# A GNN attention kernel on one core: a third of the probabilities is turned through DRAM and VectorE instead of TensorE

## The chip, the cores and the metric

One core of a Trainium2 chip. The metric is the device time of one launch in microseconds (us). PE is TensorE, DVE is VectorE, ACT is ScalarE, POOL is GpSimd, SP is SyncE, whose queue issues every DMA of this kernel.

## The reference, cut to what matters

`x` is (64, 128, 384) and `adj` (64, 128, 128), all float32; 12 heads of 32 columns.

```python
h = jnp.maximum(_layernorm(x, axis=-1), 0.0)
q, k, v = split_heads(h @ Wq + bq), split_heads(h @ Wk + bk), split_heads(h @ Wv + bv)
scores = jnp.einsum('bhqd,bhkd->bhqk', q, k) / jnp.sqrt(HD)
adj_e = adj[:, None, :, :]
scores = jnp.where(adj_e > 0, scores + beta * adj_e, -9e15)
probs = jax.nn.softmax(scores, axis=-1)
out = jnp.einsum('bhqk,bhkd->bhqd', probs, v)
x = x + out.transpose(0, 2, 1, 3).reshape(B, N, D)
```

## The kernel before, in words

The 64 graphs form 16 groups of four. The program of each engine is written out by hand as a chain of slots, one graph each, `s` = 0 to 3 inside a group; `Slot` says which works a slot does, and `slots` puts groups 2 to 11 in a hardware loop for PE, ACT, SP and POOL. Four graphs are in work in each slot: one is normalised (`z.t`), one gets scores and mask (`z.a`), the one before it is exponentiated and turned (`z.e = z.a - 1`), and the one before that is multiplied by v (`z.o = z.a - 2`). Besides, a share of the q and k projections of the whole group runs in every slot.

- **PE.** A matrix product for q and k is split into high and low parts: `h_hi*w_hi`, `h_hi*w_lo`, `h_lo*w_hi` for three pieces of the depth, nine matmuls of 512 columns for each of six units (`project`; `STRETCH_1` and `STRETCH_2` say which of them stand in which slot: 13, 14, 14 and 13). `values` is the same for v (nine of 384 columns). `scores` has 12 matmuls of depth 32 into the tile S_ps, `probs_times_v` has 12 into PT_ps, and `transpose_probs(z, m)`, m = 0, 1, 2, turns four heads each by four transposes into PT_ps. A slot runs `probs_times_v`, `scores`, `transpose_probs` 0, the first stretch, `values`, `transpose_probs` 1 and 2, the second stretch.
- **DVE.** `mask` adds the bias to the scores and takes the row maximum, 12 instructions with 12 reads of the accumulator. `store_outT` transposes the result in blocks of 32 and puts it in out_blocks, `transpose_blocks` does the same for the normalised graph, and `normalise`, `reciprocals`, `quotient` (y), `add_bv` (v), `moments`, `statistics`, `mask_terms`, `mask_bias`, `low_part` (h_lo) follow. `store_qk` moves two of six projection units from PSUM (`STORE_V`).
- **ACT.** `exponentials(z, m)`, four each for m = 0, 1, 2, with the row sum; `store_probsT(z, m)` copies the turned probabilities from PSUM to probsT; `high_part` (h_hi); `store_qk` for the other four units.
- **SP.** The tiles out_blocks and xhat_blocks go to DRAM in rows and come back in four reads each, which put the blocks of 32 where a 128 by 128 transpose has them. The queue works in order: a DMA whose semaphore is late keeps all behind it waiting. x is loaded a group at a time, in slot `s` = 1, and adj in slot `s` = 0.

Only for the first two groups (`z.X`) PE turns the normalised graph itself, and only in the last slots (`z.F`) it turns the output itself. The matmuls of `warm` keep PE busy while the first inputs arrive.

## Time and profile before

| what | value |
|---|---|
| median of 3 runs | 534.79 us (534.7 to 534.97) |
| the profiled execution's own time | 535.0 us |
| its span in the trace | 533.1 us |
| busy in the span: PE, ACT, DVE, POOL | 520.9, 462.3, 451.9, 127.3 us |
| granted TensorE clock | 1.0 of full speed |
| DMA: packets, bytes | 89671 packets, 75.25 MB |

The span is the time between the first and the last record. A busy time is the union of the instructions of an engine. Where instructions are pipelined, the mean duration of one is longer than the distance between two starts, and it is this distance that adds up.

### The profile page before, as it was taken

Reading aid. Unit: us, or ns where it says so; the run is one execution under the profiler, and the core shown is the slowest. Engines: PE = TensorE matmul, PEld = TensorE weight load, DVE = VectorE, ACT = ScalarE, POOL = GpSimd, SP = SyncE. Lnnn points to the kernel's source line nnn. Section 1 sums busy time; section 2 is a strip of 40 time slices with the busy share of each in tenths; the row PEclk is TensorE's granted clock in tenths of the full one; section 3 lists DMA queues with packets and bytes.
Section 4 is the critical chain, followed back from the end, with each engine's and each line's share of the span. In section 5 each row is a group of like instructions: output and inputs, shape, how many; then the busy total and the mean of one; then the engine's idle time right before and its main releaser. Section 6 shows DMA issues by size and latency. Waiting matters only on the chain.

```text
span 533.1 us, 17434 instructions
## 1 busy us (share of the span) xinstructions
PE 520.9 (98%) x5394; PEld 438.7 (82%) x5394; DVE 451.9 (85%) x2285; ACT 462.3 (87%) x1856; POOL 127.3 (24%) x204
## 2 busy tenths in 40 slices
PE   8989999999999999999999999999999999999995
PEld 8768888888888888888888888888888888888774
DVE  6788998888898898898888889888889987765896
ACT  3558899999999999999999999998998999888984
POOL 4522222212212222221221222222122111101211
PEclk9999999999999999999999999999999999999999
DMA  7523374654646465464645556364565434222111
GB/s 238 186 81 91 115 215 123 201 154 133 192 137 188 123 170 176 123 192 140 189 134 149 177 143 192 128 188 133 138 189 161 128 116 123 71 80 75 51 56 46
DMA packets 89671, 75.25 MB, mean 141 GB/s; under 512 B 39056, under 2 KB 86288, under 8 KB 89616
## 3 DMA queue, kind: packets, MB, share of 16 engines
q1 hardware_dynamic: 89616, 74.62, 46.5%
q8 instruction: 22, 0.36, 0.3%
q14 instruction: 33, 0.27, 0.2%
HBM read 40.37 MB, written 34.21 MB: 140 GB/s over the span
## 4 chain that ended last, share of the span: by engine, by line
PE 90%; DVE 2%; issue 1%; DVEq 0%
PE G_ps L797 35%; PE S_ps L868 18%; PE PT_ps L852 17%; PE S_ps L817 10%; PE PT_ps L834 9%; DVE probsT L682 1%; DVE probs L651 0%; PE G_ps L852 0%; PE PT_ps L858 0%; DVE outT L634 0%; PE S_ps L878 0%; DVE y L701 0%; PE S_ps L894 0%; DVE y L669 0%; DVE qk L621 0%
## 5 line engine op out<-in xcount | busy, mean ns | idle before, releaser
L481 ACT ACTIVATE probs<-probs,negmax 128x128 f32<-128x128 f32 x768 | 298.1, 397 | 0.1
L651 DVE CUSTOM_DVE_ANT_0 probs<-S_ps,bias 128x128 f32<-128x128 f32 x768 | 164.2, 283 | 3.3 <-PE S_ps L817 3.3
L481 ACT ACTIVATION_READ_ACCUMULATOR probs<-probs,negmax 128x1 f32 x768 | 150.2, 196 | 0.0
L452 POOL TENSOR_TENSOR y<-y,x_ring 128x384 f32<-128x384 f32 x63 | 63.4, 1007 | 343.6 <-DVE y L669 343.6
L797 PE MATMUL G_ps<-h_hi,w_lo 128*128 128x512 f32 x288 | 117.7, 409 | 0.0
L797 PE MATMUL G_ps<-h_hi,w_hi 128*128 128x512 f32 x288 | 117.7, 409 | 0.0
L797 PE MATMUL G_ps<-h_lo,w_hi 128*128 128x512 f32 x288 | 116.2, 403 | 0.0
L489 ACT COPY probsT<-PT_ps 128x512 f32<-128x512 f32 x181 | 99.9, 584 | 12.0 <-PE PT_ps L852 11.4
L852 PE MATMUL PT_ps<-ident,probs 128*128 128x128 f32 x728 | 103.6, 277 | 0.0
L852 PEld LDWEIGHTS PT_ps<-ident,probs 128*128 128x128 f32 x728 | 81.9, 141 | 10.3 <-issue 1.0
L868 PE MATMUL S_ps<-w_hi,h_hi 128*128 128x384 f32 x192 | 65.2, 339 | 0.0
L629 DVE STREAM_TRANSPOSE out_blocks<-PT_ps 128x384 f32<-128x384 f32 x58 | 33.8, 583 | 36.9 <-PE PT_ps L834 34.9
L868 PE MATMUL S_ps<-w_hi,h_lo 128*128 128x384 f32 x192 | 64.6, 336 | 0.0
L868 PE MATMUL S_ps<-w_lo,h_hi 128*128 128x384 f32 x192 | 64.5, 336 | 0.0
L651 DVE DVE_READ_ACCUMULATOR2_ANT negmax<- 128x1 f32 x768 | 64.1, 84 | 0.0
L817 PE MATMUL S_ps<-qk 32*128 32x128 f32 x1536 | 61.3, 287 | 2.7 <-DVE h_lo L590 2.5
L797 PEld LDWEIGHTS G_ps<-h_hi,w_hi 128*128 128x128 f32 x288 | 54.3, 189 | 10.0 <-issue 0.2
L797 PEld LDWEIGHTS G_ps<-h_lo,w_hi 128*128 128x128 f32 x288 | 54.3, 189 | 9.5
L817 PEld LDWEIGHTS S_ps<-qk 32*128 32x128 f32 x1536 | 48.8, 185 | 16.1 <-issue 14.2
L797 PEld LDWEIGHTS G_ps<-h_hi,w_lo 128*128 128x128 f32 x288 | 54.4, 189 | 8.7
L834 PEld LDWEIGHTS PT_ps<-probsT,v 128*32 128x32 f32 x1512 | 37.5, 109 | 25.1 <-issue 25.0
L834 PE MATMUL PT_ps<-probsT,v 128*32 128x128 f32 x1512 | 54.3, 277 | 3.4 <-DVE probsT L682 3.4
(57 smaller groups left out, 603.6 us busy)
## 6 DMA issues: line engine op xcount, KB each, us to landing
out_dram<-y SPq DMA_DIRECT2D x63, 192.0 KB, 1.9
x_ring<-in_x_dram SPq DMA_DIRECT2D x15, 768.0 KB, 5.4
out_rows<-out_blocks SPq DMA_DIRECT2D x58, 192.0 KB, 1.9
out_moved<-out_rows SPq DMA_DIRECT2D x232, 48.0 KB, 2.1
xhat_rows<-xhat_blocks SPq DMA_DIRECT2D x26, 384.0 KB, 2.6
xhat_moved<-xhat_rows SPq DMA_DIRECT2D x104, 96.0 KB, 2.7
adj_in<-in_adj_dram SPq DMA_DIRECT2D x16, 256.0 KB, 3.2
x_ring<-in_x_dram SPq DMA_DIRECT2D x4, 192.0 KB, 3.2
```

Source lines behind the costliest of these rows:

```text
L452: nc.gpsimd.tensor_tensor(y[:, z.s % 2 ^ d, :], y[:, z.s % 2 ^ d, :], x_ring[:, bass.ds(at, D)], ALU.add).then_inc(y_ready, 1)
L481: last = nc.scalar.activation(p, p, ACT.Exp, bias=negmax[:, e, j * KC + m:j * KC + m + 1], scale=TURN, accum_out=rowsum[:, e, m * HC + j:m ...
L489: nc.scalar.copy(probsT[:, m, :], pT_bank(z, m)).then_inc(pT_stored[m], 1)
L629: nc.vector.transpose(out_blocks[:, :].rearrange("p (b m d) -> p m b d", b=HC, m=KC), outT_ps.rearrange("p (m b e) -> p m b e", m=KC, b=HC ...
L651: last = nc.vector.tensor_tensor_reduce(probs[:, a, j, m, :], S_ps[:, j, m * N:(m + 1) * N], bias[(z.par + 1) % 2][:, z.s, :], 1.0, LARGES ...
L682: nc.vector.tensor_copy(probsT[:, m, :], pT_bank(z, m)).then_inc(pT_stored[m], 1)
L797: mm = nc.tensor.matmul(G_ps[:, u % 2, :], pairs[n][0], pairs[n][1], start=(n == 0), stop=(n == len(pairs) - 1))
L817: last = nc.tensor.matmul(S_ps[:, j, m * N:(m + 1) * N], qk_a[rs, m, ts], qk_a[rs, KC + m, ts], start=True, stop=True, tile_position=(j * ...
L834: last = nc.tensor.matmul(outT_ps[j * HD:(j + 1) * HD, m * N:(m + 1) * N], v[:, z.s % 2, h * HD:(h + 1) * HD], probsT[:, h // HC, h % HC * ...
L852: last = nc.tensor.transpose(pT_bank(z, m)[:, j * N:(j + 1) * N], probs[:, (z.s - 1) % 2, j, m, :], ident[:, :])
L868: last = nc.tensor.matmul(v_ps, hh, ww, start=(n == 0), stop=(n == len(pairs) - 1))
```

## The change: what it does

1. The four heads m = 0 of each graph no longer go through `transpose_probs(z, 0)` on PE and `store_probsT(z, 0)` on ACT. `exponentials_ahead` computes them one slot earlier (graph `z.a`, behind its mask) and writes them to probs_blocks. SP writes these to DRAM (probs_rows, 256 KB), and in the next slot reads them back in four DMAs of 64 KB into probs_moved. DVE transposes the 32 by 32 blocks into probsT (`transpose_probs` on DVE, 128 by 512). This is so for graphs 0 to 58; the last five go as before.
2. Outside slot `s` = 0 PE runs `scores` ahead of `probs_times_v`, and DVE runs `reciprocals` and `mask` ahead of `store_outT`. `scores` waits for `h_lo_stored` in the first two groups, and elsewhere in slot 0 alone.
3. ACT's copies of m = 1 and 2 stand behind `exponentials_ahead`, `high_part` behind the copies. Of six projection units ACT stores five, DVE one.
4. x is loaded graph by graph (`LOADS`) at the end of SP's slots 0, 1 and 2, adj at the end of slot 1.
5. At the start the four first graphs are loaded ahead of the weights, PE's `warm` has 22 matmuls in place of 30, and `low_part` and the low weights stand elsewhere. In the last slots the copies are shared out anew between DVE and ACT.

The core of the diff:

```diff
+LOADS = [[0], [1, 2], [3], []]
 STORE_1 = [[], [1], [], [4]]
 STORE_2 = [[0], [], [3], []]
-STORE_V = [[], [2], [], [5]]
-WARM = [8, 4, 4, 6, 8]
+STORE_0 = [[], [], [2], []]
+STORE_V = [[], [], [], [5]]
+WARM = [8, 2, 2, 3, 7]
...
+        FOUR = HC * HD
+        probs_blocks = sb("probs_blocks", [P, HC * FOUR])
+        probs_rows = nc.dram_tensor("probs_rows", [2, P, HC * FOUR], F32, kind="Internal").ap()
+        probs_moved = sb("probs_moved", [P, 2, HC * FOUR])
...
@@ sync, start
-            for q in range(2):
+            for q in range(GROUP):
                 load_first(q)
             load_weights(0, wq, 0, P, w_first)
-            for q in range(2, GROUP):
-                load_first(q)
             load_weights(0, wq, P, D, w_loaded[0])
+            load_first(GROUP)
...
@@ sync, slot
+                if z.R:
+                    sp.wait_ge(probs_rows_written, 16 * (z.e + 1))
+                    for c in range(HC):
+                        came = probs_rows[(z.s - 1) % 2, :, c * FOUR:(c + 1) * FOUR].rearrange("(r p) n -> p r n", r=HC)
+                        goes = probs_moved[c * HD:(c + 1) * HD, (z.s - 1) % 2, :].rearrange("p (r n) -> p r n", r=HC)
+                        sp.dma_start(goes, came).then_inc(probs_blocks_moved[(z.s - 1) % 2], 16)
...
+                if z.Q:
+                    sp.wait_ge(probs_ready[0], z.a + 1)
+                    sp.dma_start(probs_rows[z.s % 2, :, :], probs_blocks[:, :]).then_inc(probs_rows_written, 16)
...
+                if z.T and z.s == 1:
+                    if started(z.groups(0)):
+                        sp.wait_ge(bias_ready, z.count(0) - 1)
+                    sp.dma_start(adj_in[(z.par + 1) % 2][:, :, :],
...
+                    for q in LOADS[z.s]:
+                        sp.dma_start(x_ring[:, bass.ds(z.ring(3, q), D)],
...
@@ scalar
+            def exponentials_ahead(z):
+                act.wait_ge(masked, z.a + 1)
+                if started(z.a - 1):
+                    act.wait_ge(rinv_ready, z.a - 1)
+                if started(z.a):
+                    act.wait_ge(probs_rows_written, 16 * z.a)
+                a = z.s % 2
+                blocks = probs_blocks.rearrange("p (c j e) -> p j c e", c=HC, j=HC)
+                for j in range(HC):
+                    last = nc.scalar.activation(blocks[:, j, :, :], probs[:, a, j, 0, :].rearrange("p (c e) -> p c e", c=HC), ACT.Exp,
+                                                bias=negmax[:, a, j * KC:j * KC + 1], scale=TURN, accum_out=rowsum[:, a, j:j + 1])
+                last.then_inc(probs_ready[0], 1)
...
@@ vector
+            def transpose_probs(z):
+                dve.wait_ge(probs_blocks_moved[(z.s - 1) % 2], 64 * (z.moved_before() + 1))
+                if started(z.e):
+                    dve.wait_ge(pv_done, z.e)
+                nc.vector.transpose(probsT[:, 0, :].rearrange("p (j r e) -> p r j e", j=HC, r=HC),
+                                    probs_moved[:, (z.s - 1) % 2, :].rearrange("p (r j e) -> p r j e", r=HC, j=HC)).then_inc(pT_stored[0], 1)
...
+                if z.O and not z.F:
+                    reciprocals(z)
+                if z.scores_first:
+                    mask(z)
                 if z.O:
                     store_outT(z)
+                if z.A and not z.F and not z.scores_first:
+                    mask(z)
...
@@ tensor
-                pe.wait_ge(h_lo_stored, z.t)
+                if z.X or z.M and z.s == 0:
+                    pe.wait_ge(h_lo_stored, z.t)
...
+                if z.A and z.scores_first:
+                    scores(z)
                 if z.O:
                     probs_times_v(z)
-                if z.A:
+                if z.A and not z.scores_first:
                     scores(z)
-                if z.E:
-                    transpose_probs(z, 0)
```

The first place is PE's program in slot `s` = 1 of the loop, with its waits. Before, from `probs_times_v` (PT_ps<-probsT,v) to the first matmul of `project` (G_ps):

```order
L834 MATMUL PT_ps<-probsT,v 32x128 [waits pT_stored2,v_stored]
L834 MATMUL PT_ps<-probsT,v 32x128 x11
L807 REGISTER_ALU [waits v_stored,masked]
L817 MATMUL S_ps<-qk 128x128 [waits h_lo_stored]
L817 MATMUL S_ps<-qk 128x128 x11
L852 MATMUL PT_ps<-ident,probs 128x128 [waits pT_stored2,probs_ready0]
L852 MATMUL PT_ps<-ident,probs 128x128 x3
L797 MATMUL G_ps<-h_hi,w_lo 128x512
```

And of the change:

```order
L913 MATMUL S_ps<-qk 128x128 [waits v_stored,masked]
L913 MATMUL S_ps<-qk 128x128 x11
L929 MATMUL PT_ps<-probsT,v 32x128 [waits pT_stored2,pT_stored0,v_stored]
L929 MATMUL PT_ps<-probsT,v 32x128 x11
L892 MATMUL G_ps<-h_hi,w_lo 128x512
```

The four transposes of m = 0 are gone, the scores stand first and no longer wait for the low part, and the product with v waits for DVE's transpose (pT_stored0).

The second place is DVE's program between two masks, in one slot of the loop. Before:

```order
L669 TENSOR_TENSOR y<-out_moved,rinv 128x384 [waits out_written0,out_blocks_moved0,rinv_ready]
L676 TENSOR_TENSOR v<-S_ps,bv_rows 128x384 [waits pv_done,v_in_psum]
L563 BN_STATS bn<-x_ring 128x6
L599 TENSOR_SCALAR mask_term<-adj_in 128x128 [waits bias_ready]
L567 BN_AGGR meanvar<-bn 128x2 [waits bn6_ready]
L607 SCALAR_TENSOR_TENSOR bias<-adj_in,beta_turned,mask_term 128x128 [waits mask_ready]
L590 SCALAR_TENSOR_TENSOR h_lo<-hT,h_hi 128x3x128 [waits h_hi_stored]
L618 TENSOR_SCALAR qk<-G_ps,bq_scaled 128x512 [waits scores_in_psum,qk_in_psum]
L629 STREAM_TRANSPOSE out_blocks<-PT_ps 128x3x4x32 [waits out_rows_written,pv_done]
L585 STREAM_TRANSPOSE hT<-xhat_moved 128x4x3x32 [waits blocks_moved1]
L579 TENSOR_SCALAR xhat_blocks<-x_ring,meanvar,rstd 128x4x96 [waits rstd_ready]
L640 RECIPROCAL rinv<-rowsum 128x12 [waits normalised,probs_ready2]
```

And of the change, from behind a mask to the next:

```order
L704 STREAM_TRANSPOSE out_blocks<-PT_ps 128x3x4x32 [waits out_rows_written,pv_done]
L660 STREAM_TRANSPOSE hT<-xhat_moved 128x4x3x32
L654 TENSOR_SCALAR xhat_blocks<-x_ring,meanvar,rstd 128x4x96 [waits rstd_ready]
L744 TENSOR_TENSOR y<-out_moved,rinv 128x384 [waits out_written0,out_blocks_moved0,rinv_ready]
L751 TENSOR_TENSOR v<-S_ps,bv_rows 128x384 [waits pv_done,v_in_psum]
L764 STREAM_TRANSPOSE probsT<-probs_moved 128x4x4x32 [waits pv_done,probs_blocks_moved0]
L638 BN_STATS bn<-x_ring 128x6
L674 TENSOR_SCALAR mask_term<-adj_in 128x128 [waits bias_ready]
L642 BN_AGGR meanvar<-bn 128x2 [waits bn6_ready]
L682 SCALAR_TENSOR_TENSOR bias<-adj_in,beta_turned,mask_term 128x128 [waits mask_ready]
L665 SCALAR_TENSOR_TENSOR h_lo<-hT,h_hi 128x3x128 [waits h_hi_stored]
L715 RECIPROCAL rinv<-rowsum 128x12 [waits normalised,probs_ready2]
```

The transposes of the output and of the graph now stand behind the mask, a new transpose waits for the four reads of probs_moved, and the unit q2 of the projection (L618) is ACT's.

The third place is SP's queue in slots `s` = 1 and 2 of the loop. Before, slot 1 and the start of slot 2:

```order
L369 DMA out_rows<-out_blocks 128x384 [waits outT_stored]
L380 DMA x_ring<-in_x_dram 128x4x384
L355 DMA xhat_rows<-xhat_blocks 128x768 [waits xhat_ready]
L397 DMA out_moved<-out_rows 32x4x96 [waits out_rows_written]
L397 DMA out_moved<-out_rows 32x4x96 x3
L401 DMA out_dram<-y 128x384
```

And of the change, from the write of the new rows in slot 1 to their reads in slot 2:

```order
L419 DMA probs_rows<-probs_blocks 128x512 [waits probs_ready0]
L425 DMA out_moved<-out_rows 32x4x96 [waits out_rows_written]
L425 DMA out_moved<-out_rows 32x4x96 x3
L429 DMA out_dram<-y 128x384
L435 DMA adj_in<-in_adj_dram 128x4x128
L443 DMA x_ring<-in_x_dram 128x384
...
L402 DMA probs_moved<-probs_rows 32x4x128 [waits probs_rows_written]
L402 DMA probs_moved<-probs_rows 32x4x128 x3
```

Between the write and its reads stand the four reads of the output, the store of y and, in slot 1, three loads.

## Rows read from the trace of the kernel before

**Rows 1.** The page: busy time of each engine.

```profile
PE 520.9 (98%) x5394; PEld 438.7 (82%) x5394; DVE 451.9 (85%) x2285; ACT 462.3 (87%) x1856; POOL 127.3 (24%) x204
```

**Rows 2.** The page: the chain that ended last, by engine.

```profile
PE 90%; DVE 2%; issue 1%; DVEq 0%
```

**Rows 3.** Busy time in one group's four slots (PE, PEld, DVE, ACT, POOL, clock, DMA, GB/s).

```profile
218.85:250.22 31.37, 31.37 (x332) 26.44 (x331) 27.63 (x144) 28.87 (x118) 7.86 (x12) 1.00 0.53 159
```

**Rows 4.** Timeline of PE in one slot (start, duration).

```profile
255.69 0.86 PE L834 MATMUL PT_ps<-probsT,v 128*32 128x128 f32 x24
256.49 0.95 PE L817 MATMUL S_ps<-qk 32*128 32x128 f32 x24
257.37 0.66 PE L852 MATMUL PT_ps<-ident,probs 128*128 128x128 f32 x4
257.78 0.48 PE L797 MATMUL G_ps<-h_hi,w_lo 128*128 128x512 f32 x1
258.10 0.40 PE L797 MATMUL G_ps<-h_lo,w_hi 128*128 128x512 f32 x1
258.34 0.39 PE L797 MATMUL G_ps<-h_hi,w_hi 128*128 128x512 f32 x1
```

**Rows 5.** The page: groups of instructions that the change removes or resembles.

```profile
L852 PE MATMUL PT_ps<-ident,probs 128*128 128x128 f32 x728 | 103.6, 277 | 0.0
L489 ACT COPY probsT<-PT_ps 128x512 f32<-128x512 f32 x181 | 99.9, 584 | 12.0 <-PE PT_ps L852 11.4
L629 DVE STREAM_TRANSPOSE out_blocks<-PT_ps 128x384 f32<-128x384 f32 x58 | 33.8, 583 | 36.9 <-PE PT_ps L834 34.9
```

**Rows 6.** Groups by line, DVE, whole span.

```profile
L585 DVE STREAM_TRANSPOSE hT<-xhat_moved 128x384 f32<-128x384 f32 x52 | 27.9, 536 | 0.0
L618 DVE TENSOR_SCALAR qk<-G_ps,bq_scaled 128x512 f32<-128x512 f32 x16 | 12.0, 751 | 7.4 <-PE G_ps L797 7.3
```

**Rows 7.** Timeline of DVE from one mask on (start, duration).

```profile
250.35 0.23 DVE L651 CUSTOM_DVE_ANT_0 probs<-S_ps,bias 128x128 f32<-128x128 f32 x1
...
252.83 0.55 DVE L669 TENSOR_TENSOR y<-out_moved,rinv 128x384 f32<-128x384 f32 x1
253.53 0.56 DVE L676 TENSOR_TENSOR v<-S_ps,bv_rows 128x384 f32<-128x384 f32 x1
...
256.62 0.58 DVE L629 STREAM_TRANSPOSE out_blocks<-PT_ps 128x384 f32<-128x384 f32 x1 [0.95 <-PE PT_ps L834]
257.13 0.53 DVE L585 STREAM_TRANSPOSE hT<-xhat_moved 128x384 f32<-128x384 f32 x1
257.59 0.44 DVE L579 TENSOR_SCALAR xhat_blocks<-x_ring,meanvar,rstd 128x384 f32<-128x384 f32 x1
```

**Rows 8.** Timeline of ACT: copies, a unit, the first of the exponentials.

```profile
253.53 0.53 ACT L511 ACTIVATE h_hi<-hT 128x384 fp32r<-128x384 f32 x1 [0.99 <-PE S_ps L868]
253.97 1.07 ACT L489 COPY probsT<-PT_ps 128x512 f32<-128x512 f32 x2
254.93 0.70 ACT L497 ACTIVATE qk<-G_ps,bq_scaled 128x512 f32<-128x512 f32 x1
255.51 0.41 ACT L481 ACTIVATE probs<-probs,negmax 128x128 f32<-128x128 f32 x1
...
257.05 0.40 ACT L481 ACTIVATE probs<-probs,negmax 128x128 f32<-128x128 f32 x1
```

**Rows 9.** Timeline of SP's queue: issues (start, duration, how many).

```profile
236.19 1.98 SPq L397 DMA_DIRECT2D out_moved<-out_rows  x4
239.06 0.36 SPq L401 DMA_DIRECT2D out_dram<-y  x1
...
250.08 0.39 SPq L374 DMA_DIRECT2D adj_in<-in_adj_dram  x1
```

**Rows 10.** DMAs into out_moved: time from issue to landing.

```profile
DMA to landing us min/median/max: 1.8/2.1/5.3
```

**Rows 11.** Who waited for whom on PE, first 60 us (us, times, longest).

```profile
PE S_ps L817 <- DVE h_lo L590: 2.5, 2, 1.3
```

More of the change, by code:

```diff
@@ L154, in gnn_attention @@
         bq_ready, beta_ready = sem("bq_ready"), sem("beta_ready")
-        x_first = [sem(f"x_first{i}") for i in range(GROUP)]
+        x_first = [sem(f"x_first{i}") for i in range(GROUP + 1)]
         x_loaded = [sem(f"x_loaded{i}") for i in range(2)]
@@ L209, in __init__ @@
                 self.L = self.O and not self.E
+                self.R = self.E and not self.F
+                self.Q = self.A and self.P and not (n == NG - 1 and s == GROUP - 1)
                 self.W = self.O and not self.F
@@ L213, in __init__ @@
                 self.moved, self.turned = [1] * before, [0] * (self.F and self.O and not self.L)
+                self.between = self.A or s == GROUP - 1
+                self.scores_first = self.A and self.P and s > 0
                 self.par = off % 2
@@ L287, in pT_bank, with transposed, loads @@
                 return (PT_ps[:, 0, :], G_ps[:, 0, :], G_ps[:, 1, :])[m]
-            return PT_ps[:, m % 2, :]
+            return PT_ps[:, m - 1, :]
+        def transposed(z, m):
+            return z.e + 1 - (B - GROUP - 1 if m == 0 else 0)
+        def loads(g):
+            return 64 * (g // 2) if g % 2 == 0 else 64 * (g // 2) + 16
         def started(count):
@@ L443, in slot @@
                         deviation(s, s)
+                    pool.wait_ge(w_lo_dve, 1)
                     weights_low(1)
@@ L514, in slot @@
             def slot(z):
+                if z.L:
+                    act.wait_ge(third_pv, KC)
+                    nc.scalar.copy(outT[:, (KC - 1) * N:], outT_last(KC - 1)).then_inc(third_outT[KC - 1], 1)
                 if z.T and not z.P:
@@ L517, in slot @@
                 if z.E:
-                    exponentials(z, 0)
+                    if z.F:
+                        exponentials(z, 0)
                     exponentials(z, 1)
-                    if not (z.F and not z.A):
+                    if z.F and z.A:
                         store_probsT(z, 0)
+                if z.P:
+                    for u in STORE_0[z.s]:
+                        store_qk(z, u)
+                if z.E:
                     exponentials(z, 2)
+                    if z.F and not z.A:
+                        store_probsT(z, 2)
                 if z.P:
@@ L525, in slot @@
                         store_qk(z, u)
-                if z.M:
-                    high_part(z)
+                if z.Q:
+                    exponentials_ahead(z)
                 if z.E and not z.F:
                     store_probsT(z, 1)
-                if z.X and z.A:
+                if z.X and z.P and z.between:
                     high_part(z)
@@ L533, in slot @@
                     store_probsT(z, 2)
+                if z.M:
+                    high_part(z)
                 if z.P:
-                    for u in STORE_2[z.s]:
+                    for u in STORE_2[z.s] + STORE_V[z.s] * (z.static and z.groups(0) == 0):
                         store_qk(z, u)
-                if z.X and z.P and not z.A:
+                if z.X and z.P and not z.between:
                     high_part(z)
@@ L615, in store_qk @@
                 if u < KC:
-                    if z.static and z.groups(0) == 0:
+                    if z.static and z.groups(0) == 1:
                         dve.wait_ge(bq_ready, 1)
@@ L714, in slot @@
                                 normalise(z, q - 1)
+                        low_part(z)
                         normalise(z, GROUP - 1)
@@ L727, in slot @@
                     normalise(z, q)
-                if z.O:
+                if z.F and z.O:
                     reciprocals(z)
-                if z.A and not z.F:
-                    mask(z)
                 for d in z.moved:
@@ L765, in slot @@
                     normalise(z, q)
-                if z.P:
+                if z.P and not first:
                     for u in STORE_V[z.s]:
                         store_qk(z, u)
+                if first and z.s == GROUP - 1:
+                    weights_low(8)
             all_slots(slot)
@@ L936, in slot @@
                     transpose_probs(z, 1)
-                if z.X and z.A:
+                if z.X and z.P and z.between:
                     transpose_xhat(z)
@@ L943, in slot @@
                         project(z, *part)
-                if z.X and z.P and not z.A:
+                if z.X and z.P and not z.between:
                     transpose_xhat(z)
```

121 lines of the change are left out of this document (60 added, 61 removed).

## The prediction

> **What bounds the kernel now.** I read the busy times first: PE is busy 98% of the span, ACT 87%, DVE 85% [rows 1]. The chain that ended last agrees: 90% of it is PE [rows 2]. Then one group's four slots from the middle: in 31.37 us PE has no idle time at full clock, DVE works 27.63 and ACT 28.87 [rows 3]. So a slot takes 31.37/4 = 7.84 us, because PE's work takes that long, and only what leaves PE shortens it. But DVE has just 3.7 us of room in a group, and the change gives DVE work. The question is which of the two sets the new slot, and whether the new way through DRAM keeps up.
>
> **PE: what a removed transpose is worth.** The page gives 277 ns as the mean of one transpose [rows 5]. That is its length in the pipeline; the distance between starts adds up. In the timeline the four transposes of m = 0 start at 257.37 and the next matmul at 257.78: 0.41 us for all four [rows 4]. The G matmul behind them takes 0.32 to the next start, where the one after takes 0.24; I take this extra 0.08 as the price of passing from the short matmuls to the long ones. It stays, since the product with v now stands at that place, and would be gained only if it belonged to the transposes alone (then 0.49). Swapping scores and product keeps PE's work. A group's PE work becomes 31.37 - 4 x 0.41 = 29.73 us, 7.43 a slot.
>
> The Trainium skill (TensorE: Matmul & The Clock Gate, Part 4: PE-mode transpose) reports about 275 ns for a 128x128 transpose in a kernel's context. By that price the four would give 1.1 us and the 59 graphs 65 us; the trace's mean agrees with the page, and its start distances say that this price must not be summed.
>
> **DVE: what it gets and loses.** The new transpose is 128x512 from SBUF. The nearest row is the 128x384 one, 536 ns long [rows 6], and 257.59 - 257.13 = 0.46 from start to start [rows 7]. Scaled by 4/3 it occupies 0.61; the upper bound is the whole duration scaled, 0.71. I take 0.61, as it stands between other DVE work. DVE loses one projection unit a group, 0.75 [rows 6]. Its work becomes 27.63 - 0.75 + 4 x 0.61 = 29.32 us a group (29.72 with 0.71), just under PE's 29.73. Its waits for PE at out_blocks (34.9 us in all [rows 5]) must vanish, or DVE would not fit: they do, since the mask, 252.83 - 250.35 = 2.48 us [rows 7], now stands between the scores and that transpose, and the product with v takes only 0.80 [rows 4]. Both engines run without room, and PE needs DVE's masks and qk unit at the group boundary, so I charge some friction below.
>
> **ACT** loses a copy a slot, about 0.48 (two start 0.96 apart, 253.97 to 254.93), and gains one unit a group, 0.58 (254.93 to 255.51) [rows 8]: 28.87 - 1.9 + 0.6 = 27.5 of 29.7. It has room, and is only on the path of the new round trip.
>
> **The round trip.** For each graph: ACT's four exponentials, a write, four reads, DVE's transpose, and then the product in the slot after. I walk through the worst slot. T0 to T3 are the ends of the scores in slots 0 to 3. PE's interval T0 to T1 is 7.43 less the product (0.80, which in slot 0 stands before the scores and in slot 1 behind) less half a long matmul (0.12): 6.5. T1 to T2 and T2 to T3 are 7.43 + 0.12 = 7.55. In slot 0 the mask ends at T0 + 2.5. ACT then has four exponentials (1.54: 255.51 to 257.05), two copies 0.96, high_part 0.44, unit 0 (0.58), eight exponentials 3.1, unit 1 (0.58), and the four of the next graph 1.54 [rows 8]: T0 + 11.3, about T1 + 4.8. From there SP issues the write 0.36, the output's four reads 1.98, y 0.36, adj 0.39, two x loads 0.8 and three of the four new reads 1.5, with six gaps of some 0.1 [rows 9], and the last read lands 2.1 us after its issue (median [rows 10]): 8.1 us, T1 + 12.9 = T2 + 5.35. DVE comes to its transpose after mask 2.48, out_blocks 0.51, hT 0.46, xhat 0.44, y 0.55 and v 0.56 [rows 7]: T2 + 5.0. So it waits 0.35 us there. In the other slots no more than one load stands in the way; the transpose finds its data, with half a microsecond to a few tenths to spare. DVE's own room, 29.73 - 29.32, could take up all of this wait (bound: nothing), but PE also waits for DVE's unit 5 at the boundary, which could double it (bound: 0.7). I charge 0.3 a group: 29.73 + 0.3 = 30.0 us, 7.50 to 7.51 a slot.
>
> **SP's queue** has 36 issues a group now and 59 then (16 reads, 4 writes, 3 more x loads). Reads take up to 0.5 each, the others 0.36 to 0.41 [rows 9]: 40 x 0.5 + 19 x 0.38 = 27 of 30 us. It fits without much room. **The DMA engines** are 53% busy at 159 GB/s [rows 3], 5.0 MB a group. The change adds 4 x 0.52 MB: at equal efficiency 0.53 x 31.37/30.0 x 7.1/5.0 = 79%. This fits too, but landings can grow. x in four pieces rather than one of 768 KB works against that.
>
> **Small edits.** That the scores no longer wait for h_lo costs and brings nothing in the middle, where PE does not wait. In the first two groups two such waits cost PE 2.5 us [rows 11]; low_part stands earlier there, and I credit 2 us of it. Fewer warm-up matmuls and earlier x loads, and the new shares of the last copies, I put at 0.5 together (bounds: 0 and 2, as nothing but a first matmul or a tail copy moves). Sum: 2.5 us.
>
> **The sum.** 59 graphs go the new way, each saving (31.37 - 30.0)/4 = 0.34: 20.2 us. With 2.5: 535.0 - 22.7 = 512.3 us for the profiled execution, whose own time is 0.2 above the median of the runs: 512.
>
> **The rivals.**
> - *The transposes were worth more* (chance 0.09). If the 0.08 behind them goes as well, PE's group is 31.37 - 4 x 0.49 = 29.41, still above DVE's 29.32. With no wait for the round trip that saves 0.49 x 59 = 28.9, and with the edges 2.5: 503.5 us. Against it speaks that other short matmuls then precede the same long one.
> - *The round trip is late and gives part back* (0.16). It closes a loop over two slots: exponentials to transpose, on average some 7.4 us (8.1 in the worst slot); then the rest of DVE's slot with the transpose, 7.33 - 5.0 = 2.3, the next mask 2.48 and the exponentials 1.54, 6.3 in all. (7.4 + 6.3)/2 = 6.9 a slot stays hidden under 7.43. If every landing took 1.5 us more than the median, it would be 7.6: 0.24 x 59 + 2.5 = 16.7 less, 518; with 1.9 more, 7.8: 530. For it: 79% busy DMA engines, and a longest landing of 5.3 [rows 10].
> - *The round trip decides, and the kernel is slower* (0.05). Same place, same loop: from a landing of 4.1 us on (7.84 x 2 - 13.7 = 2.0 above the median) the slot is longer than before. At 4.6 it is (9.9 + 6.3)/2 = 8.1: 535 + 0.26 x 59 - 2.5 = 548. Against it: the median of 2.1 includes landings behind other transfers. The Trainium skill (DMA: Bandwidth & Descriptors, Latency and other measured facts) puts the access to DRAM at 0.2 us on average and 2 us at high load. If 79% were such a load, write and reads would each land 1.8 later, the loop would be 17.3 and the slot 8.65, some 580 us. No row here shows a queue in that state for long.
> - *Nothing comes of it* (0.02): PE finds a new wait in each slot, for DVE's masks or pT_stored0, of about the 0.41 saved: 533 to 536.
>
> **How the numbers follow.** The forecast, 507 to 516, has 0.68: 29.73 a group and the edges of 4.5 give 535 - 24.2 - 4 = 507 at one end, DVE's transpose at 0.71 and the wait twice as long, with no edges, give 516 at the other. The first rival below it and the better half of the second reach 505 and 521, which leaves out the worst of both, the slower rival and the last. A change within 0.2% (1.1 us) can't be told from none here. Faster: 0.68 + 0.09 + 0.16 = 0.93; same 0.02; slower 0.05.
>
> **What would show it right or wrong.** PE's four-slot period should be 29.7 to 30.2, with PE idle for some tenths at the group's boundary, waiting for qk or masks from DVE. DVE should be 97% or more busy in the middle, its new transpose some 0.67 us long, waiting for probs_moved in slot 2 of a group alone, for a few tenths. The wait at out_blocks should be gone. SP's queue should be some 90% occupied and the reads of probs_moved land in 2.1 to 2.6. I am wrong if DVE waits for probs_moved in every slot, if landings exceed 3.6 in the median, if the new transpose takes over 0.8, or if the starts on PE show that the missing transposes left their time behind.

## The result and the profile after

547.87 us (median of four, 546.83 to 551.03; the ratio also counts a fifth, 544.11) against 534.79 before on the same chip: ratio 1.0238, 95% interval 1.017 to 1.0306, so 13 us slower where 23 less were forecast. Executions more than 1.5% above the fastest of their kernel are in no median, range or ratio of this text: one of 605.17 before, and in the tables below one of loads_spread_on_act (542.27) and two of x_whole_on_act (553.78 and 557.26). The profiled execution took 551.03, its span is 548.9. The page's busy times and, below, the chain that ended last, one of its costliest groups and two of its DMA groups:

```profile
PE 507.4 (92%) x5142; PEld 418.8 (76%) x5142; DVE 467.3 (85%) x2323; ACT 443.0 (81%) x1816; POOL 127.0 (23%) x204
...
DMA packets 132840, 106.20 MB, mean 193 GB/s; under 512 B 44464, under 2 KB 121904, under 8 KB 132784
...
SPq 38%; PE 19%; DMA 12%; DVE 10%; issue 8%; ACT 3%; DVEq 0%; ACTq 0%
...
L764 DVE STREAM_TRANSPOSE probsT<-probs_moved 128x512 f32<-128x512 f32 x59 | 41.8, 709 | 43.3 <-DMA probs_moved<-probs_rows 43.2
...
probs_rows<-probs_blocks SPq DMA_DIRECT2D x59, 256.0 KB, 2.8
probs_moved<-probs_rows SPq DMA_DIRECT2D x236, 64.0 KB, 2.3
```

PE is busy 13.5 us less than before [rows 1]; the forecast took 59 x 0.41 = 24.2 from it, and in no_trip_at_all below, where PE hardly stops, it is 23.2. The chain, which was 90% PE [rows 2], now lies half on SP's queue and the DMAs, and DVE stands 43 us waiting for probs_moved. One group's four slots in the middle and the PE rows at its end (start, duration, in brackets the idle time before):

```profile
263.84:295.64 31.80, 30.24 (x314) 25.00 (x315) 28.88 (x146) 26.92 (x112) 7.57 (x13) 1.00 0.73 223
```

```profile
285.63 0.95 PE L913 MATMUL S_ps<-qk 32*128 32x128 f32 x24
286.88 0.86 PE L929 MATMUL PT_ps<-probsT,v 128*32 128x128 f32 x24 [0.30 <-issue]
...
294.14 0.86 PE L929 MATMUL PT_ps<-probsT,v 128*32 128x128 f32 x24 [0.62 <-DVE probsT L764]
295.64 1.09 PE L913 MATMUL S_ps<-qk 32*128 32x128 f32 x24 [0.64 <-DVE h_lo L665]
```

A group takes 31.80 us [rows 3: 31.37], with PE idle for 1.56 of it. From scores to scores the slots take, in the median of groups 2 to 13 (the first is 0), 6.67, 7.56, 7.56 and 10.04 us; before 7.73, 7.97, 7.96 and 7.72. Three slots are as forecast (6.5, 7.55, 7.55); all is lost in the last, where 8.1 was forecast, or 8.4 with the 0.3 of friction. SP's queue and DVE around the transpose of slot 2 in the same group, whose scores are at 278.07:

```profile
276.81 0.32 SPq L419 DMA_DIRECT2D probs_rows<-probs_blocks  x1
277.48 1.82 SPq L425 DMA_DIRECT2D out_moved<-out_rows  x4
279.48 0.36 SPq L429 DMA_DIRECT2D out_dram<-y  x1
280.04 0.41 SPq L435 DMA_DIRECT2D adj_in<-in_adj_dram  x1
280.66 0.94 SPq L443 DMA_DIRECT2D x_ring<-in_x_dram  x2
281.72 1.78 SPq L402 DMA_DIRECT2D probs_moved<-probs_rows  x4
283.54 0.43 SPq L406 DMA_DIRECT2D out_rows<-out_blocks  x1
```

```profile
283.59 0.55 DVE L751 TENSOR_TENSOR v<-S_ps,bv_rows 128x384 f32<-128x384 f32 x1
286.06 0.71 DVE L764 STREAM_TRANSPOSE probsT<-probs_moved 128x512 f32<-128x512 f32 x1 [1.92 <-DMA probs_moved<-probs_rows]
...
294.96 0.55 DVE L665 SCALAR_TENSOR_TENSOR h_lo<-hT,h_hi 128x384 fp32r<-128x384 f32 x1
295.43 0.75 DVE L696 TENSOR_SCALAR qk<-G_ps,bk_col 128x512 f32<-128x512 f32 x1
```

SP goes from the write to the reads with no pause over 0.35 us, the last read goes out at about 283.1 and has landed at 286.06, and DVE has stood since 284.14. Between there and the group's end it idles for only another 0.2 us, so it cannot catch up, and h_lo and the qk unit, for which PE's next scores wait, come late. PE's wait is seen where the delay ends, not where it begins.

Below, "waits by graph" are DVE's waits for probs_moved in groups 2 to 13, each transpose put to the slot of its graph. In the changed kernel they are, for slots 0 to 3, 1.1, 6.1, 21.0 and 5.9 us, and slot 2 waits in 12 of 12 groups. I first assigned them by where PE stood; so the expectations of loads_late, tiny_trip_waited and one_read_loads_late speak of slot 3 where slot 2 is meant. "Occupied" is SP's issuing between 100 and 440 us, the sum of its rows; the expectations have it up to 5 us higher, because I had counted rows at the edges of short windows twice.

### The profile page after: what moved, and what is told of

Read it like the earlier page. It is cut to its first block, busy times and chain, and to the rows that moved or that the text cites. A ratio compares the mean times of both kernels' runs of the same rounds, so it can differ in the third digit from the quotient of the medians.

```text
span 548.9 us, 17414 instructions
## 1 busy us (share of the span) xinstructions
PE 507.4 (92%) x5142; PEld 418.8 (76%) x5142; DVE 467.3 (85%) x2323; ACT 443.0 (81%) x1816; POOL 127.0 (23%) x204
## 4 chain that ended last, share of the span: by engine, by line
SPq 38%; PE 19%; DMA 12%; DVE 10%; issue 8%; ACT 3%; DVEq 0%; ACTq 0%
SPq L425 12%; SPq L402 11%; DMA out_rows<-out_blocks 8%; PE G_ps L892 7%; PE S_ps L961 4%; SPq L429 4%; SPq L443 4%; PE S_ps L913 4%; SPq L394 4%; DMA probs_moved<-probs_rows 4%; DVE probs L726 4%; PE PT_ps L945 2%; PE PT_ps L929 2%; ACT probs_blocks L542 2%; SPq L419 1%
## 5 line engine op out<-in xcount | busy, mean ns | idle before, releaser
L527 ACT ACTIVATE probs<-probs,negmax 128x128 f32<-128x128 f32 x532 | 206.0, 397 | 0.0
L542 ACT ACTIVATE probs_blocks<-probs,negmax 128x128 f32<-128x128 f32 x236 | 91.9, 393 | 71.9 <-DVE negmax L726 71.8
L892 PE MATMUL G_ps<-h_hi,w_hi 128*128 128x512 f32 x288 | 120.1, 417 | 0.0
L527 ACT ACTIVATION_READ_ACCUMULATOR probs<-probs,negmax 128x1 f32 x532 | 105.0, 197 | 0.0
L764 DVE STREAM_TRANSPOSE probsT<-probs_moved 128x512 f32<-128x512 f32 x59 | 41.8, 709 | 43.3 <-DMA probs_moved<-probs_rows 43.2
L913 PEld LDWEIGHTS S_ps<-qk 32*128 32x128 f32 x1536 | 50.9, 188 | 33.8 <-issue 32.3
L913 PE MATMUL S_ps<-qk 32*128 32x128 f32 x1536 | 63.9, 294 | 11.8 <-DVE h_lo L665 11.4
L550 ACT COPY probsT<-PT_ps 128x512 f32<-128x512 f32 x122 | 64.9, 579 | 6.9 <-PE PT_ps L945 6.3
L945 PE MATMUL PT_ps<-ident,probs 128*128 128x128 f32 x492 | 66.2, 273 | 0.0
```

Source lines behind the costliest of these rows:

```text
L527: last = nc.scalar.activation(p, p, ACT.Exp, bias=negmax[:, e, j * KC + m:j * KC + m + 1], scale=TURN, accum_out=rowsum[:, e, m * HC + j:m ...
L542: last = nc.scalar.activation(blocks[:, j, :, :], probs[:, a, j, 0, :].rearrange("p (c e) -> p c e", c=HC), ACT.Exp, bias=negmax[:, a, j * ...
L550: nc.scalar.copy(probsT[:, m, :], pT_bank(z, m)).then_inc(pT_stored[m], 1)
L892: mm = nc.tensor.matmul(G_ps[:, u % 2, :], pairs[n][0], pairs[n][1], start=(n == 0), stop=(n == len(pairs) - 1))
L913: last = nc.tensor.matmul(S_ps[:, j, m * N:(m + 1) * N], qk_a[rs, m, ts], qk_a[rs, KC + m, ts], start=True, stop=True, tile_position=(j * ...
L945: last = nc.tensor.transpose(pT_bank(z, m)[:, j * N:(j + 1) * N], probs[:, (z.s - 1) % 2, j, m, :], ident[:, :])
```

## The experiments

Kernels that leave out part of the way of the probabilities: no_trip_at_all has no write and no reads, tiny_trip and tiny_trip_waited write 8 KB and read 4 x 2 KB, quarter_bytes writes 64 KB and reads 4 x 16 KB, the rest of DVE's transpose being constant data; no_wait_for_reads and one_read_no_wait move all bytes and do not use them; the three with one read bring the rows in another order. All others compute everything.

### What the trip costs, step by step

| kernel | us (range) | ratio, 95% | groups in the middle | occupied | DMA share |
|---|---|---|---|---|---|
| no_trip_at_all | 514.21 (513.78 to 514.52) | 0.958 to 0.962 | 30.1 | 189 | 0.54 |
| tiny_trip | 515.24 (514.34 to 515.7) | 0.961 to 0.964 | 30.1 | 265 | 0.55 |
| tiny_trip_waited | 519.85 (519.47 to 520.26) | 0.968 to 0.973 | 30.1 to 30.9 | 261 | 0.55 |
| one_read_no_wait | 524.22 (522.39 to 528.39) | 0.975 to 0.986 | 30.1, once 33.5 | 232 | 0.76 |
| quarter_bytes | 533.69 (532.1 to 534.89) | 0.995 to 0.998 | 31.1 | 285 | 0.59 |
| no_wait_for_reads | 535.78 (533.42 to 538.35) | 0.999 to 1.003 | 31.1 | 286 | 0.74 |
| changed kernel | 547.87 | 1.017 to 1.031 | 32.1 | 280 | 0.72 |

**quarter_bytes**

```diff
-came = probs_rows[(z.s - 1) % 2, :, c * FOUR:(c + 1) * FOUR].rearrange("(r p) n -> p r n", r=HC)
+came = probs_rows[(z.s - 1) % 2, 0:HD, c * FOUR:(c + 1) * FOUR]
...
-sp.dma_start(probs_rows[z.s % 2, :, :], probs_blocks[:, :])
+sp.dma_start(probs_rows[z.s % 2, 0:HD, :], probs_blocks[0:HD, :])
```

> The changed kernel with the new round trip cut to a quarter of its bytes: one write of 64 KB and four reads of 16 KB per graph, at the same places and with the same waits; three quarters of the turned probabilities of the first four heads are left out. Theory Q (SP's queue is the bound: its issues and its own waits fill about 32 us a group): 59 issues a group stay, so the time stays within 4 us of 547.9 and the median landing of the reads may fall without effect. Theory B (DMA bytes: landings are late because the engines are 70% busy): the DMA share falls to about 55%, DVE's 43 us of waiting for probs_moved mostly go, and the time falls to 515 to 525.

Three quarters of the bytes gone brought 14 of the 34 us by which the changed kernel is above no_trip_at_all, so neither theory alone holds. Its DVE still waits 19.0 us by graph, 11.8 of it in slot 2.

**no_wait_for_reads**, **no_trip_at_all**, **tiny_trip**: DVE takes a constant tile; then the write and reads go as well; then four rows of each come back.

```diff
-dve.wait_ge(probs_blocks_moved[(z.s - 1) % 2], 64 * (z.moved_before() + 1))
...
-    probs_moved[:, (z.s - 1) % 2, :].rearrange(...)
+    probs_still[:, :].rearrange(...)
```

> The changed kernel with every write and read of the round trip as it is, but DVE transposes a constant tile and waits for no read; the probabilities of the first four heads are replaced by zeros. Theory W: DVE never waits for the trip, a group takes 29.8 to 30.3, 511 to 518 us. Theory Q: SP is as busy as before and holds ACT (which waits until probs_rows is written) and y, 535 or more. Bytes alone slowing the other engines would show as longer instructions on DVE, ACT or PE.

> As the one before, and the write and the four reads are left out too: the four heads' probabilities are computed and dropped, the rest of the kernel is whole. This is what the change would be worth with a free round trip. All theories: PE is the bound, 29.7 to 29.9 us a group, 508 to 513 us. If it is over 516, something else than the trip holds the new order of the slots.

> As no_wait_for_reads (DVE transposes a constant tile), with the write and the four reads at their places and with their waits, but each moves 4 rows: 8 KB written and 2 KB per read in place of 256 and 64 KB. It stands between no_trip_at_all (514.2) and no_wait_for_reads (535.8), which differ by issues and bytes both. Theory Q (the time that SP's queue takes per issue): the issues are all there, 528 to 536, with SP issuing over 270 of 340 us in the middle. Theory B (bytes and packets): they are gone, 514 to 518.

Without the trip the kernel is where the forecast was. no_wait_for_reads came out at theory Q's lower bound, and tiny_trip as theory B had it. The page of no_trip_at_all, then SP's waits between 100 and 440 us (total, times, longest) in it and in no_wait_for_reads:

```profile
PE 497.7 (97%) x5142; PEld 413.4 (81%) x5142; DVE 466.7 (91%) x2323; ACT 443.3 (86%) x1816; POOL 128.0 (25%) x205
```

```profile
SPq L402 <- DVE out_blocks L698: 85.8, 45, 4.2
SPq L418 <- DMA out_rows<-out_blocks: 18.5, 24, 2.2
```

```profile
SPq L427 <- DMA out_rows<-out_blocks: 17.7, 25, 1.1
```

Without the trip SP is ready 86 us before DVE; with it, it waits for nothing but a landing in its own order. There 286.4 us of issuing, 26.3 of gaps under 0.25, these 17.7 and some 10 of longer pauses, in which SP waits for nothing that the profile shows, fill the 340: the queue is full, at 31.1 us a group. The full queue makes other transfers late. In no_wait_for_reads between 100 and 440 us:

```profile
ACT probs_blocks L547 <- DMA probs_rows<-probs_blocks: 12.1, 10, 3.1
DVE y L749 <- issue: 12.3, 11, 3.2
```

Each of the 11 waits at y ends 0.1 us after the last read of the output (out_moved) has landed. I took tiny_trip at first for proof that the number of issues costs nothing. It isn't: reads of four rows go out 0.335 us apart, those of 32 rows 0.47, so it also left SP 22 us.

**one_read_no_wait** keeps the bytes and takes three issues of four away; **tiny_trip_waited** keeps the issues and the wait and takes the bytes away.

```diff
-for c in range(HC): ...                          # four reads of 64 KB
+came = probs_rows[(z.s - 1) % 2, :, :].rearrange("(r q) n -> r (q n)", r=HC).rearrange("r (p n) -> p r n", p=P)
+goes = probs_moved[:, (z.s - 1) % 2, :].rearrange("p (r n) -> p r n", r=HC)
```

> Leaves out the use of what is read: DVE transposes a constant tile and does not wait, and the one read of 256 KB (in place of four of 64 KB) brings the rows in another order. All bytes travel: the write of 256 KB and the read of 256 KB for each graph, 12 issues a group fewer on SP. Theory Q (SP's queue is full, 291 of 340 us issuing with four reads, 218.6 with one): SP has room, the middle groups fall to 30.1 to 30.3 and the whole to 514 to 518. Theory B (the bytes make the other landings late): DMA share stays 0.73 to 0.75, middle groups 30.8 to 31.5, the whole 528 to 537.

> Leaves out nearly all of the probabilities' way: 8 KB written and four reads of 2 KB in each slot, and DVE transposes a constant tile, but waits for the four reads as the changed kernel does. Without that wait it took 515.2, SP issued for 268 of 340 us and its reads in slot 3 began 2.9 us behind the scores (4.3 in the changed kernel). Theory Q: the wait finds the reads landed in nearly all slots, DVE waits under 4 us between 100 and 440 and the whole is 515 to 520. Theory O (it is the order, exponentials to write to the other reads to these reads, whatever is on the queue and the engines): DVE waits 10 us and more, 524 to 532.

With all bytes on the engines (0.76 of their time) but room on SP the middle groups take 30.1 us: in steady state bytes alone cost PE nothing. The 10 us over no_trip_at_all lie in groups 1 and 2 (32.9 and 32.4 us for 30.0 and 30.1) and in a few later ones. The total is thus between both expectations. In tiny_trip_waited DVE waits 8.1 us by graph in slot 2, 0.68 a group, and 0.5 elsewhere; its total is at the upper end of theory Q.

Three pairs of kernels now differ in whether DVE waits for the trip. In groups 3 to 13 the changed kernel waits 29.1 us and takes 10.3 us longer than no_wait_for_reads; one_read waits 27.1 and takes 15.6 longer than one_read_no_wait; tiny_trip_waited waits 7.6 and takes 2.2 longer than tiny_trip. So 0.3 to 0.6 us are paid for each us that DVE waits, and not the whole.

### Other queues, other places

| kernel | us (range) | ratio, 95% | waits by graph, slots 0 to 3 | occupied |
|---|---|---|---|---|
| changed kernel | 547.87 | 1.017 to 1.031 | 1.1, 6.1, 21.0, 5.9 | 280 |
| write_on_act | 542.46 (540.2 to 543.16) | 1.012 to 1.016 | 0, 0.6, 12.4, 2.1 | 270 |
| stores_loads_on_pool | 545.02 (544.56 to 546.85) | 1.017 to 1.022 | 0, 2.7, 13.6, 6.1 | 245 |
| both_moved | 547.46 (544.49 to 548.83) | 1.017 to 1.025 | 0, 1.0, 11.5, 4.7 | 225 |
| late_transpose | 547.21 (545.62 to 549.36) | 1.020 to 1.027 | 0, 0, 0.4, 0.5 | 281 |
| one_read | 546.44 (544.53 to 549.55) | 1.019 to 1.026 | 0.6, 0.8, 27.9, 0.9 | 214 |
| one_read_loads_late | 539.11 (535.08 to 541.6) | 1.004 to 1.009 | 12.6, 0, 12.9, 1.7 | 227 |
| loads_late | 540.07 (538.96 to 544.2) | 1.007 to 1.013 | 7.5, 4.0, 13.7, 2.3 | 289 |
| slot_1_without_loads | 547.21 (544.48 to 549.94) | 1.019 to 1.025 | 12.5, 8.2, 1.4, 11.3 | 281 |
| loads_on_act | 532.98 (530.05 to 537.05) | 0.993 to 1.000 | 4.2, 2.9, 4.7, 2.7 | 275 |
| loads_spread_on_act | 537.05 (533.42 to 540.64) | 1.000 to 1.005 | 0.3, 11.8, 3.1, 8.9 | 269 |
| x_whole_on_act | 547.85 (544.33 and 551.36) | 1.014 to 1.030 | 28.1, 0.9, 2.0, 3.8 | 253 |

**write_on_act**, **stores_loads_on_pool**, **both_moved**: the write issued by ACT behind `exponentials_ahead`; y, adj and x issued by POOL; both.

```diff
-sp.dma_start(probs_rows[z.s % 2, :, :], probs_blocks[:, :])    # SP, slot
+act.dma_start(probs_rows[z.s % 2, :, :], probs_blocks[:, :])   # ACT, behind exponentials_ahead
```

> The changed kernel with the write of probs_rows issued by ACT right behind its four exponentials, all else the same. Theory Q: SP loses four issues of 0.4 us a group and 9 to 12 us of waits in all, and the write starts up to 1.5 us earlier; DVE's wait for the reads shrinks in part: 533 to 541. Theory B: bytes are the same, 545 to 549.

> The changed kernel with y's stores and the loads of x and adj issued by POOL: 9 of 59 issues a group leave SP's queue (4.1 us at 0.46 each with the gaps between them). Theory Q: SP's cycle falls from some 32 to 28 us a group, below PE's 29.7, and the time falls to 515 to 525, with a group's period of 29.8 to 30.5. Theory B: no gain, 544 or more. A third outcome, POOL's own issues taking so long that the normalisation is late, would show as DVE waiting for rstd or for y.

> Both edits: the write on ACT, the stores and loads on POOL; SP keeps 46 of 59 issues. Theory Q: PE is the bound again, a group takes 29.7 to 30.0 us, and the time is 510 to 516, the number forecast for the change. Theory B: 540 or more.

write_on_act misses theory Q's 533 to 541 by 1.5 us and is 5 faster than the changed kernel; the other two are 20 and 31 above Q's 515 to 525 and 510 to 516. What uses up SP's relief, between 100 and 440 us in both_moved:

```profile
PE PT_ps L930 <- ACT probsT L549: 4.8, 7, 0.8
```

```profile
SPq L423 <- DMA out_rows<-out_blocks: 38.1, 36, 2.5
SPq L403 <- DMA probs_rows<-probs_blocks: 22.7, 21, 2.0
```

ACT stands 0.46 us in each slot until the write is out, its copies come later, and PE waits for them. SP has room, but stands for the landings of out_rows and of the trip's own write before it may issue their reads, and DVE still waits 17.2 us by graph for the trip. Loads that POOL issues land 3.9 us after their issue instead of 2.9. So a full queue is not the whole cause: with SP issuing for 225 of 340 us the reads still come late.

**late_transpose**: DVE's transpose behind `low_part`.

```diff
-if z.R:
-    transpose_probs(z)        # behind add_bv
...
     low_part(z)
+if z.R:
+    transpose_probs(z)
```

> The changed kernel with DVE's transpose of probs_moved moved behind low_part in the same slot, some 1.9 us later; nothing else. Theory W (the round trip of 8 to 9 us misses its place in DVE's program by up to 2.7 us, and DVE, with almost no room, passes each wait on to the group's boundary): the waits for probs_moved (29 us in the middle of the kernel) go, a group takes 30.0 to 30.6 us in place of 31.6 to 33, and the time is 513 to 522. Theory Q (SP's queue, with 27 us of issues, 2 of gaps and its own waits, can't be quicker than some 31.5 us a group): the waits only move, and the time stays at 540 or more.

DVE's wait is gone and the kernel no faster: the products in slot 1 and in slot 0, where the product stands ahead of the scores, now wait for the later transpose. Slot 1 takes 8.43 us for 7.56, and slot 3, counted up to the scores of slot 0 and so with that product, 9.29. Each stands 11 times between 100 and 440 us, 9.4 and 12.6 us in all. One wait was exchanged for another.

**one_read** (the diff above, with DVE's wait)

> The changed kernel with one read of 256 KB per graph in place of four of 64 KB, in the same 512-byte pieces, so that the bytes and packets stay; the blocks land in another order, so the first four heads' probabilities are permuted. DVE waits for this read as before. 12 of 59 issues a group go. Theory Q: SP has 5.5 to 6.5 us a group of room more, its floor falls to 26 us and the trip gets 1.4 us shorter: PE is the bound, 30.0 to 30.4 us a group, 513 to 519 us. Theory B: 540 or more, and the read lands much later than 2.3 us.

It frees SP and gains nothing. The one read of 256 KB lands 3.1 us after its issue in the median, but 4.9 in slot 2, and slot 2 alone waits 27.9. Room on SP does not help a transfer that is late by its place and its landing.

**loads_late**, **one_read_loads_late**, **slot_1_without_loads**: only the places of the loads in SP's queue.

```diff
-LOADS = [[0], [1, 2], [3], []]     # adj in slot 1
+LOADS = [[], [0], [], [1, 2, 3]]   # adj in slot 1: loads_late, one_read_loads_late
+LOADS = [[0], [], [1], [2, 3]]     # adj in slot 3: slot_1_without_loads
```

> The whole computation, same issues on SP, same bytes; only the places of the x loads in SP's queue change: x of graph 0 in slot 1 and x of graphs 1 to 3 at the end of slot 3, instead of one in slot 0, two in slot 1, one in slot 2 (adj stays in slot 1). In the changed kernel 22.3 of the 29.1 us that DVE waits for probs_moved between 100 and 440 us lie in slot 3, where SP's reads start a median of 4.3 us behind the scores' start (1.0 in slot 0, 3.0 in slot 1, 3.9 in slot 2). Theory Q (SP's queue in order: its backlog grows from slot 0 to slot 3, and slot 3's reads come too late): reads of slot 3 start about 1.5 us earlier, DVE's waits fall to 8 to 14, the middle groups to 30.8 to 31.4 and the whole to 534 to 541. Theory B (the bytes on the DMA engines, 72% busy): nothing changes, 545 to 550, DVE waits 26 to 32.

> One read of 256 KB in place of four, which brings the rows in another order (the probabilities are not the reference's), DVE waits for it; x of graph 0 is loaded in slot 1, x of 1 to 3 at the end of slot 3. One read alone stayed at 546.4 with 26.8 of its 27.9 us of waits in slot 3, and the late loads alone brought 547.9 to 540.1. Theory Q (place in SP's queue): the two add, DVE waits under 10 us in 340, middle groups 30.2 to 30.9, the whole 524 to 534. Theory B (the landings under load): 538 to 546.

> The whole computation, same issues and bytes on SP: x 0 in slot 0, x 1 in slot 2, adj, x 2 and x 3 at the end of slot 3, nothing in slot 1 (the changed kernel has adj and two loads there). Counted by graphs, and not by where PE stands, the changed kernel's transpose waits 21.0 of 34.1 us in slot 2 of groups 2 to 13, in 12 of 12 groups, and starts a median of 8.0 us behind the start of that slot's scores (5.9 in the slots without a wait); its reads begin 3.75 us behind them. Theory Q (the reads of slot 2 stand behind slot 1's three loads, 1.3 us of issues, in a full queue): reads of slot 2 begin 1 to 1.5 us earlier, the wait in slot 2 falls from 1.75 to 0.3 to 0.8 a group, some of it comes back in slot 0, the middle groups take 30.8 to 31.3, the whole 535 to 540. Rival F (the queue is full anyway, 59 issues in 31 us, so that places don't matter): slot 2 starts at 7.7 or later, 541 to 547. As with the loads late (540.1), which had adj and one x in slot 1.

Places decide which slot waits. With slot 1 free of loads slot 2's wait falls from 21.0 to 1.4 us, as said, but slots 0, 1 and 3 take it over, and the sum, 33.4 against 34.1, and the time stay. A load moved is here a wait moved. loads_late has a smaller sum, 27.4, and is 7.8 us faster, within theory Q's range, though DVE waits 23.9 us between 100 and 440 where 8 to 14 were said. Both edits together, one_read_loads_late, do not add up: 539.11 against 540.07, with 27.2 us of waits, nearly half of them in slot 0, as theory B had it.

**loads_on_act**, **loads_spread_on_act**, **x_whole_on_act**: ACT issues adj and x ahead of `exponentials_ahead`.

```diff
+([0, 1], [], [2, 3], [])[z.s]   # adj in slot 0: loads_on_act
+([0], [], [1, 2], [3])[z.s]     # adj in slot 1: loads_spread_on_act
+one DMA of 768 KB in slot 0      # adj in slot 0: x_whole_on_act
```

> The changed kernel, its whole computation, with the loads of x and adj issued by ACT just before exponentials_ahead, where ACT waits for masks (two x loads and adj in slot 0, two x loads in slot 2); SP keeps 54 of 59 issues. Theory Q: SP's floor falls by 2.5 to 3 us a group to about 28.8, below PE: 30.2 to 31 us a group, 516 to 528. Theory B: 543 or more.

> The whole computation. As the kernel whose loads ACT issues, but with one load in slot 0 (x 0), adj in slot 1, x 1 and 2 in slot 2 and x 3 in slot 3, instead of adj, x 0 and x 1 together in slot 0 and x 2 and 3 in slot 2. There the middle groups took 30.1 to 30.9 us and the first three 38.1, 34.1 and 32.3, against 32.9, 30.0 and 30.1 without the round trip; a write of probs_rows took 4 us there behind xhat_rows and two x loads, the DVE stood 2.3 us, PE 3.1, and the clock fell to 0.71 of full speed for 10 us. Theory L (bursts of loads beside a write make the first groups late, and the clock adds to it): first groups 34, 32 and 31, middle 30.1 to 30.5, the whole 523 to 529. Theory S (the first groups are late whatever the loads do, as SP's program is denser there): first groups as they were, 530 to 535.

> The whole computation. As the kernel whose loads ACT issues (532.98, five issues a group on ACT), but x of a group goes in one DMA of 768 KB, issued by ACT in slot 0 beside adj: two issues a group on ACT, 54 on SP as there. Theory Q (ACT's and SP's queues, not the bytes): ACT gets 3 x 0.46 us a group back, middle groups stay at 30.1 to 30.6, the whole 528 to 533. Theory B (a large transfer beside the trip makes its landings late, as 768 KB took 5.4 us to land before the change): DVE waits 20 us and more between 100 and 440, 536 to 545.

loads_on_act is the fastest version that computes everything: the sum of waits is 14.5, groups 4 to 12 take 30.1 to 30.9 us, and against before it gains 0.4% (interval 0.05 to 0.7), far from theory Q's 516 to 528. Spreading the loads made it worse, against my expectation. What a load beside the reads does is seen in the last read's landing in loads_on_act, in the median of each slot: 3.67 us in slot 0, with adj and two x loads beside it, 2.85 in slot 2 with two, 1.97 and 2.09 in slots 1 and 3 with none. x_whole_on_act has it larger. SP's reads and ACT's load go out together (timelines of SP and ACT), and DVE waits; behind its row stands that of the landings of probs_moved from 226 to 250 us:

```profile
235.38 1.88 SPq L403 DMA_DIRECT2D probs_moved<-probs_rows  x4
```

```profile
235.35 0.46 ACTq L594 DMA_DIRECT2D x_ring<-in_x_dram  x1
```

```profile
243.96 0.71 DVE L761 STREAM_TRANSPOSE probsT<-probs_moved 128x512 f32<-128x512 f32 x1 [3.36 <-DMA probs_moved<-probs_rows]
```

```profile
DMA to landing us min/median/max: 2.0/2.2/7.1
```

The longest landing, 7.1, is beside the load; the median is 2.2. In slot 0 these waits are 28.1 us; in the three slots with no load beside the reads, with the trip's full bytes, 0.9, 2.0 and 3.8. (The profiled execution is its longest, 557.26 at a mean clock of 0.972, so its rows are used for these waits and not for the total.)

## Why the prediction was wrong

- **PE's saving: right.** Without the trip 514.21 us against 512 forecast, the group 30.1 against 30.0, its slots 6.67, 7.56, 7.56 and 8.30 against 6.5, 7.55, 7.55 and 8.1 to 8.4. The 0.08 behind the transposes stayed. DVE's transpose is 0.709 long and the next instruction starts 0.64 behind it (286.06 to 286.70), where 0.61 was forecast; it fits. Starts and ends came to 2.0 us (first scores 26.88 for 28.32, and 0.5 at the end) of the 2.5.
- **The step that failed first** is the round trip's: "8.1 us, T1 + 12.9 = T2 + 5.35", "so it waits 0.35 us there". Slot and DVE's arrival were right: in the rows above the scores of slot 2 end at 279.0 and DVE is ready at 284.14, T2 + 5.1. But the last read went out at T2 + 4.1, not 3.25, since the write is issued half a microsecond later and SP also waits in order for out_rows to land; and it landed 3.0 later, not 2.1. That is T2 + 7.0, a wait of 1.92 (mean over 12 groups 1.75). The medians of these groups say the same: the write at T1 + 5.3 for 4.8, the last read out at T2 + 4.15 and landed 2.7 later, while the last reads of the other slots land in 2.05 to 2.16. I had the terms of the queue, but priced the one landing that has three loads just ahead of it at the median of an engine load of 0.53.
- **What it costs.** Slot 3 takes 10.04 instead of 8.30, 1.74 more, where I had bounded the effect by 0 to 0.7. It is tempting to equate this with the 1.75 of waiting in slot 2, but that is luck: with the wait taken away (no_wait_for_reads) slot 3 still takes 9.29. So the queue costs 1.0 a group and the wait 0.75 more. In tiny_trip_waited, with the same wait, shorter issues and hardly a byte, slot 2 waits 0.68, slot 3 takes 8.37 and the kernel 519.85: of the 33.7 us above no_trip_at_all 5.6 are left.
- **"27 of 30 us. It fits without much room": the second step that failed.** Issuing is 26 a group, but gaps (2.4), longer pauses (0.9) and in-order waits for landings (1.6), which the sum left out, make it 31.1 in no_wait_for_reads, more than PE's 30.1. In one order of removal: 514.2, with all bytes in one read 524.2, with four reads 535.8, with DVE's wait 547.9. The parts depend on the order, since one_read with its wait is at 546.4. In the spans of the profiled executions the changed kernel is 36.0 above no_trip_at_all: 13.8 in groups 0 to 2 and 22.0 in groups 3 to 13, and of these no_wait_for_reads keeps 9.6 and 11.7.
- **"The DMA engines 79%. This fits too": half right.** 0.76 of their time did not slow the middle groups where SP had room and nobody waited for the trip; but single landings became longer, and loads beside the reads decide which slot waits.
- **The rivals.** The sum was nearest the one that "decides, and the kernel is slower", 548, but not by its mechanism: it wanted landings of 4.1 us in every slot, and the median was 2.3. Late reads in one slot and a full queue were enough. (The range's lower end, 507, takes 4 off for edges that it calls 4.5; nothing hangs on it.) The rule cited with it from the Trainium skill (DMA: Bandwidth & Descriptors, Latency and other measured facts), 2 us of access at high load in place of 0.2, would have made the median landing 1.8 longer; the trace has 2.3 for 2.1, and single reads of up to 3.8 here and 7.1 in x_whole_on_act, so such a state is not seen in the median.
- **The first groups** cost 13.8 of these 36.0 us: they take 36.2, 36.3 and 34.2 us, where no_trip_at_all takes 32.9, 30.0 and 30.1. There the clock is also lower behind a stall. PE after 2.57 us of waiting:

```profile
53.47 1.44 PE L913 MATMUL S_ps<-qk 32*128 32x128 f32 x24 [2.57 <-DVE h_lo L665]
54.84 1.51 PE L929 MATMUL PT_ps<-probsT,v 128*32 128x128 f32 x24
```

The same matmuls take 0.95 and 0.86 later; the granted clock between 50 and 60 us is 0.83, so for a third of that time it was at the lower of its two levels, 1.2 GHz instead of 2.4. It is 0.83 again in 80 to 90, 230 to 240 and 390 to 400 us, behind idle times of PE of 1.99, of 1.07 and 0.64, and of 1.03 and 0.77. Together that is some 14 us at the lower level: by my estimate from these rows at most 7 of the 36.0 us are the clock's. The mean clock of no_trip_at_all is 1.0. Which transfers make these groups late stays open: loads moved to ACT left them at 38.0, 34.1 and 32.3.

## What to carry to other kernels

Before a trip through DRAM is put beside a tight engine, write out the in-order queue of one whole period with its gaps and with every landing that it waits for; when issues, gaps and landings fill the period, it is the new bound, whatever the engines' shares say. Price the landing of the critical transfer with what flies beside it, not by the median of a calmer kernel, and keep large loads off its moment. Ask of each wait what can absorb it before the next common point: with DVE idle for 15 of 340 us (no_trip_at_all) little does, and the delay shows on another engine one slot later. And when a wait and a loss come out equal, take the wait away before calling it the cause.

## What the hardware showed beside that

- An issue's length hardly goes with its bytes: from one read to the next 0.335 us with 4 rows of 512 bytes (2 KB), 0.46 with 16 KB and 0.47 with 64 KB in 32 rows; the one issue of 256 KB in 128 rows lasts 0.38.
- A second hardware queue shares the engines at once: a 768 KB load on ACT's queue took 8.1 us to land (5.4 on SP's before) and held reads issued beside it for 7.1. The Trainium skill (DMA: Bandwidth & Descriptors, Queues, rings and completion order) has each DMA engine take turns between the queues that have work for it; these rows fit that, though they do not show the turns themselves.
- ACT pays for what it issues: 0.33 to 0.46 us each (in write_on_act 0.33 for the write, with 0.46 from its last exponential to its next instruction), plus what it waits for ahead of the issue.
